# Value product ahead of the transposed scores of four-head units, in the slots where sixteen-head scores run

## What is computed

```
xn = layernorm(x)
x  = x + causal attention(xn), 16 heads of 8, keys and values through a 32-wide latent
       + mixture of 8 experts, the best 2 of each row (xn)
xn = layernorm(x)
ctx = attention(xn), 16 heads of 8, scores times a sigmoid gate
ctx = 0.3 ctx + 0.7 attention(xn), 4 heads of 32          ("ca" in the kernel)
ctx = 0.85 ctx + 0.15 attention(ctx), 4 heads of 32       ("mc" in the kernel)
x  = x + ctx @ Wo + gated network of width 512 (xn)
```

## Time and profile before

| | |
|---|---|
| time, median of 3 runs | 1737.87 us (1736.77 to 1743.94) |
| span of the profiled execution | 1744.8 us |
| TensorE busy | 1542.1 us (88%) |
| VectorE busy | 1199.4 us (69%) |
| ScalarE busy | 1055.2 us (60%) |
| GpSimd busy | 792.1 us (45%) |
| mean granted TensorE clock | 0.949 |

### The profile page before, as it was taken

The page is one execution under the profiler, slowest core; times in us unless marked ns, Lnnn a source line. Parts: engine busy times, 40 slices in busy tenths (PEclk is TensorE's granted clock), DMA queues, the critical chain, the costliest instruction groups (busy, mean ns, idle before and its releaser), DMA issues.

```text
span 1744.8 us, 34024 instructions
## 1 busy us (share of the span) xinstructions
PE 1542.1 (88%) x11497; PEld 656.0 (38%) x11497; DVE 1199.4 (69%) x3135; ACT 1055.2 (60%) x2322; POOL 792.1 (45%) x725
## 2 busy tenths in 40 slices
PE   3586898999999999998999999999999999889878
PEld 1353453245333543345333543345324533232232
DVE  7554478567875788667885788677876677476523
ACT  2372475667656765676666765677657765636442
POOL 5246345535645456354644455354644461501120
PEclk9998699999999999999999999999999999989877
DMA  7652451136212631136212621145212620201010
GB/s 277 205 153 69 135 158 36 57 109 176 63 34 77 167 102 48 63 115 159 63 34 87 180 79 52 62 135 145 58 46 82 186 78 7 62 15 35 1 37 6
DMA packets 138875, 159.35 MB, mean 91 GB/s; under 512 B 15744, under 2 KB 100304, under 8 KB 137808
## 3 DMA queue, kind: packets, MB, share of 16 engines
q1 hardware_dynamic: 134608, 148.79, 29.4%
q0 software_dynamic: 4096, 8.40, 1.6%
HBM read 115.96 MB, written 40.85 MB: 90 GB/s over the span
## 4 chain that ended last, share of the span: by engine, by line
PE 61%; DVE 13%; ACT 9%; issue 6%; POOL 6%; DMA 3%; SPq 2%; ACTq 0%; POOLq 0%; DVEq 0%
PE banks L454 58%; DVE negmax L879 6%; ACT probs L1222 3%; ACT hm L1291 3%; POOL psums L1443 2%; POOL xslots L1417 1%; DMA qkc<-relm 1%; DVE h L1103 1%; ACT L1222 1%; PE banks L731 1%; POOL halves L1399 1%; PE banks L684 1%; SPq L1579 1%; ACT h L1340 1%; POOL yg L1432 0%
## 5 line engine op out<-in xcount | busy, mean ns | idle before, releaser
L1222 ACT ACTIVATE probs<-banks 128x512 f32<-128x512 f32 (+3 forms) x1216 | 582.1, 535 | 371.7 <-PE banks L454 352.9
L879 DVE TENSOR_REDUCE negmax<-banks 128x1 f16<-128x512 f32 x768 | 492.2, 685 | 159.5 <-PE banks L454 156.5
L875 DVE CUSTOM_DVE_ANT_0 scr<-banks,mask_row 128x384 bf16<-128x384 f32 (+3 forms) x512 | 230.2, 487 | 150.9 <-PE banks L454 149.1
L454 PE MATMUL banks<-kp,qs 32*128 32x512 f16 (+3 forms) x1024 | 239.7, 360 | 60.4 <-DVE negmax L875 23.5
L454 PE MATMUL banks<-probs,vp 128*32 128x512 f32 (+3 forms) x2048 | 241.0, 544 | 0.2 <-POOL probs L1395 0.2
L454 PE MATMUL banks<-qs,kp 32*128 32x512 f16 (+3 forms) x1024 | 218.5, 352 | 23.2 <-ACT probs L1222 15.9
L1483 POOL TENSOR_TENSOR h_lo<-h,h_hi 128x512 f16<-128x512 f32 x96 | 114.4, 1209 | 246.4 <-ACT h_hi L1334 150.8
L1423 POOL TENSOR_TENSOR hl<-hm,hh 128x512 f16<-128x512 f32 x120 | 139.7, 1166 | 131.7 <-DVE hh L1045 131.7
L1291 ACT ACTIVATE hm<-banks,wt 128x128 f32<-128x128 f32 x480 | 137.8, 374 | 77.4 <-PE banks L454 77.0
L454 PE MATMUL banks<-qkc 97*128 97x512 f16 (+1 forms) x512 | 168.5, 402 | 8.7 <-DVE negmax L879 3.0
L454 PEld LDWEIGHTS banks<-kp,qs 32*128 32x128 f16 x1024 | 63.1, 92 | 277.5 <-DVE negmax L879 109.8
(11 more groups left out here) (212 smaller groups left out, 2462.0 us busy)
## 6 DMA issues: line engine op xcount, KB each, us to landing
wt<-wexp SPq DMA_DIRECT2D x120, 258.0 KB, 3.1
wt<-wexp SPq DMA_DIRECT2D x120, 256.0 KB, 3.0
qkc<-relm SPq DMA_DIRECT2D x96, 128.0 KB, 3.2
qs<-relq SPq DMA_DIRECT2D x64, 128.0 KB, 2.3
kp<-relk SPq DMA_DIRECT2D x64, 128.0 KB, 2.3
relm<-halves SPq DMA_DIRECT2D x32, 256.0 KB, 2.1
xg<-xslots SPq DMA_DIRECT2D x24, 256.0 KB, 3.0
yslots<-yv SPq DMA_DIRECT2D x24, 256.0 KB, 3.6
```

What stands on the lines that cost most here:

```text
L454: return nc.tensor.matmul(psum[rows_, bank, cols_], lhsT, rhs, start=start, stop=stop)
L875: v.tensor_tensor_reduce(scr[:, s, 0:kw], psum[:, SCO + s, 0:kw], mask_row[:, T - kw:T], -1.0, 3e38, ALU.add, ALU.min, negmax[:, g.n % 2, ...
L879: v.tensor_reduce(negmax[:, g.n % 2, NC * h + c:NC * h + c + 1], psum[:, SCO + s, 0:kw], AX.X, ALU.max, negate=True).then_inc(sem("max"), 1)
L1222: a.activation(keys(g, c)[:, 2 * pair + s, q0:T], psum[:, TRA + s, q0:T], ACT.Exp, scale=SCALE[main(g)]).then_inc(sem("exp"), 1)
```

## The change

In a slot where the transposed scores are of a four-head group and the scores are of a main group, trans is issued after `few_rows`, `value` and `few_cols` in place of before them. No operation is added or taken away, and no other engine's program changes.

```diff
                     turn_over(G)
                     keep_warm(G)
-                    if G in TRANS:
+                    wide_trans = G in TRANS and not main(TRANS[G][0]) and G in UNIT and main(UNIT[G][0])
+                    if G in TRANS and not wide_trans:
                         trans(*TRANS[G])
                     few_rows(G)
                     if G in VALUE_AT:
                         value(*VALUE_AT[G])
                     few_cols(G)
+                    if wide_trans:
+                        trans(*TRANS[G])
                     experts(G)
```

## The result

The changed kernel took 1755.9 us, median of five executions (1752.6 to 1759.0), against 1738.5 us for the kernel before beside it (1736.8 to 1743.9): ratio 1.0079, interval [1.0052, 1.0106]. Measured twice more (`again`, `third`) it was 1.0050 [1.0021, 1.0079] and 1.0049 [1.0027, 1.0071]. The forecast was 1743.4, or a ratio of 1.0032 by its sum of 5.5 us; 1755.9 also lies above the range. The profiled execution has a span of 1750.4 us and ran in 1752.6, the lowest of its five; that of before had been above its median, so the two spans show less of the loss than the medians. Three executions hundreds to thousands of microseconds above all others (2347.3, 5075.6 and 2110.6, one each of `again`, `base_early_table` and `no_mc_17b`) are in no comparison.

What follows compares the result with a forecast made beforehand. TensorE, busy 88% of the span, was taken to bound the kernel. Terms of +5.6 (mc), -0.6 (ca) and +0.5 us (direct ca) gave +5.5 on the 1737.9 median: 1743.4 us, range 1734 to 1751.

Steps and rivals of the forecast that it cites:

- first term: The mc mixes: transposed scores issued later wait for ScalarE's exponentials, 1.12 us per mc, five of them, +5.6 us.
- mc, unit 1: The next slot's transposed scores wait for unit 1's later exponentials, so the hidden-layer product behind starts 0.88 us late.
- S to V: TensorE's step from a slot's scores to its value product, taken as 0.32 us after the change.
- mc, units 3 to 6: Changed borders between TensorE products: unit 3 adds 0.14 us, units 4 and 5 together 0.1.
- mc, unit 7: Transposed scores come 1.0 us late, but exponentials wait behind a gelu anyway: cost 0, at most 0.5 without that cover.
- ca: -0.6 forecast: Six of seven ca: POOL's sums released 0.54 us earlier, against 0.64 us lost behind `latT`; bounds -3.8 and +4.5.
- direct ca's +0.5: Direct ca, unit 6: transposed scores move by 1.9 us and wait for exponentials; +0.5 us, bounds 0 and 1.5.
- The first (waits don't cost): Holes at mc unit 1 are made up later, delays stay hidden everywhere: total 0, 1738 us; chance 0.22.
- The second (POOL's release wins): Earlier value products gain 0.54 us in seven ca, borders 3.0, waits cost nothing: -6.8, 1731 us; chance 0.1.
- The third: In ca, ScalarE's delay at unit 4 reaches DVE's maxima: 5.6 us on top, 1749.0, or 1750.1; chance 0.18.
- signs at unit 2: In mc, unit 2's transposed scores wait about 0.6 us for ScalarE's exponentials at their first tile, five times.
- idle time of the 97-row group: Waiting of TensorE's 97-row products, the ones moved: to rise from 8.7 us by 5 to 10, released by ScalarE.

Runs made afterwards that it cites:

- base_early_table: The kernel before, old order everywhere, plus one small independent exponential on ScalarE right behind each gelu: ratio 0.9992.
- no_mc_17: The changed kernel with the old order at units 1 and 7 of the mc mixes: ratio 0.9978, and 0.9982 when measured once more.
- base: A copy of the kernel before, unchanged, run for a second profile: ratio 0.9992.
- unit7_only: The kernel before with the new order at unit 7 of the mc mixes and nowhere else: ratio 1.0047, and 1.0066 when measured once more.
- ca_only: The kernel before with the new order in the ca mixes alone: ratio 0.9988.

## Why the prediction was wrong

**Forecast missed; the mechanism of its first term was right.** Direction, place (mc, not ca) and the length of an mc stretch at full clock (1.12 forecast, 1.08 measured) held. But 1.12 came out right by luck: units 1 to 6 were put 0.77 too high and unit 7 0.74 too low. And what the lateness of unit 7 set off was not in the sum.

**mc, unit 1: 0.88 forecast, 0.66 measured.** The wait of unit 2's T is there at all five; its first tile waits 0.32 us, where "about 0.6" was said. S to V is 0.16 behind 128-wide scores (543.56 to 543.72) and not the 0.32 that was taken from a row with 512-wide ones, and T to T is 1.08, not 1.13. Together that is the difference.

**mc, units 3 to 6: +0.24 forecast; units 2 to 6 gave back 0.31 in all.** For unit 3 the forecast put T between V and `max_rows` and made the way from S to `max_rows` 1.77 us, 0.14 longer. The edit puts T behind `few_cols`, and so behind `max_rows`: S to `max_rows` is 1.10 in the changed kernel (547.90 to 549.00), against 1.63 before. With T behind it, the next full product follows S by 1.69 (547.90 to 549.59), against 1.78 before (545.84 to a product at 547.62). The border T to full product, 0.45, counts there as everywhere. The forecast set aside, for its row, the rule of the Trainium skill (TensorE: Matmul & The Clock Gate, "What overlaps and what doesn't") that a weight load overlaps products in flight only when its row group differs. The 0.31 us that came back is on the row's side.

**mc, unit 7: the step that failed.** The forecast let the wait behind the gelu cover T's delay, at a price of "0, and at most 0.5 without that cover". Measured 0.74 at each place. Up to the start of the exponentials, 947.33 in `base`, the slack looks ample: they start 2.12 us behind T. But the work that waits for T starts at 946.03 with the table load, which takes the activation's wait upon itself. In `unit7_only` the load starts 0.47 us behind T (953.21 to 953.68); in `base` it could so have started at 945.68, and the slack was 0.35 us. T itself is 1.09 later against the scores of its slot (943.03 to 945.21 before, 949.94 to 953.21 after), and 1.09 - 0.35 is the 0.74 measured. The upper bound of 0.5 rested on no row; the whole delay of T was the one to keep.

**The clock: not in the sum.** The forecast counted idle time of TensorE as its own length. Here some 0.8 us more idle time at five places of the kernel was followed, at 22 of the 35 such places in seven profiles, by a stretch at the lower clock worth twice that. This made a loss of 3.7 us one of about 8.

**ca: -0.6 forecast; a small gain, too small for the totals.** `ca_only` is 0.9988 with an interval across 1. The steps are clearer: in batch rows 1 and 5, where `base` has its full clock, the twelve ca stretches with the new order and the full clock are 0.19 to 0.46 us shorter than in `base` over sixteen slots; the same stretches with the old order differ by 0.01. Seven of that size would be 1.3 to 3.2 us (an estimate from these two rows). `latT` waits longer for DVE, as said, since T no longer stands ahead of it (timeline, TensorE, `again`; before it was 0.30):

```profile
841.87 0.60 PE L660 MATMUL banks<-const,latn 128*32 128x128 f32 x4 [0.74 <-DVE latn L1011]
```

The direct ca's +0.5 was not separated from noise.

**Rivals.** The first (waits don't cost) is out by the traces of mc. The second (POOL's release wins) is out as a total, but its first part is there: POOL waits for TensorE 48.0 to 55.7 us in the ten profiles with the new order in ca (52.1 on average) and 53.7 to 59.2 in the seven without (56.1), 4.0 less where the rival had 7 x 0.54 = 3.8. Its other part, waits that cost nothing, failed in mc. The third, which did end on the slower side, had the wrong engine and the wrong mix: ca lost nothing. None had ScalarE's table load.

**What would have shown it** named the signs at unit 2 and the idle time of the 97-row group (from 8.7 to 13.1, 12.3 and 13.6; +5 to +10 was said, and nearly met; "S to V 0.32" was not, it is 0.16). The sign that mattered was in another group (groups of ScalarE, table load of the exponential): `base`, then `unit7_only`:

```profile
L1222 ACT ACT_TABLE_LOAD x16 | 20.5, 1283 | 0.7 <-PE banks L454 0.4
```
```profile
L1225 ACT ACT_TABLE_LOAD x16 | 20.5, 1283 | 4.4 <-PE banks L454 4.2
```

**The range.** 1734 to 1751 did not hold 1755.9. The two later measurements, 1748.8 and 1746.8 us, lie inside it, beside kernels before of 1740.7 and 1738.7; the ratio of 1.005 to 1.008 is what the sum should have reached, and 5.5 us reached 1.003. The range also took 3 us for the difference between single runs, while the three runs that it had differ by 7.2 (1736.77 to 1743.94).

## What to carry to other kernels

When a product is moved behind other work, measure its slack to the first instruction of the consumer's chain that carries the wait, here the table load, and not to the activation that the load serves. A small activation of the next function right behind the last one of the other function took the load out of that chain here, for 0.2 us. A re-ordering is best tried unit by unit: the same edit here lost 0.7 us at each of two units of eight in an mc stretch and gained 0.31 at the others together, and with the old order at those two (`no_mc_17`, 0.9978 and 0.9982) it is at least not slower than the kernel before, by intervals that just reach 1.

## What was not expected of the hardware

- A table load of 1.28 us started only when the wait of the exponential behind it was met: 0.76 us of idle ahead of it in `unit7_only` and the changed kernel, none with an independent exponential between.
- TensorE's granted clock fell to 1.2 GHz at 22 of 35 places where an idle time of 1.14 us stood 4.3 us behind another of 1.14, and at 2 of 35 where the second was 0.36 us (0.45 in `base_early_table`). Each fall cost 1.2 to 1.7 us.
- An extra stretch of 51 to 58 us at the lower clock near the start takes 0.015 to 0.017 off the mean clock of an execution, and the executions with such low means are not longer. Among the others the mean clock does tell of time: in the 87 of the kernel before, 0.001 less clock goes with 1.0 us more time (correlation -0.70).
- Executions of one kernel spread by 10 to 20 us, while the mc stretches without a fall repeat within 0.05 us. Steps between two traces told what the totals needed twelve executions for.
